# One core, latent attention with a pattern branch: two program blocks joined into one, and the first slot written in another order

## The reference

```
x = x + layernorm(attn(layernorm(x)))      # x: 1 x 1024 x 256
x = x + layernorm(ffn(layernorm(x)))
attn, main branch, 16 heads:
  q = rmsnorm(h @ q_a^T) @ q_b^T           # per head 128 "nope" + 64 rotated columns
  kv_a = h @ kv_a^T                        # 64 latent columns, 16 x 64 rotated key columns
  k_nope, v = rmsnorm(latent) @ kv_b^T     # 128 + 128 per head
  main = softmax(q k^T / sqrt(192)) v, then o_w
pattern branch, 16 heads of 16 columns:
  pattern = softmax(pq pk^T / 4) pv, then sp_o_w
out = gate0 * main + gate1 * pattern       # gates = softmax over 2
ffn: two matmuls with MXFP4-quantized weights (blocks of 32), gelu between
```

## Time and profile before

| | |
|---|---|
| median of 3 runs | 828.34 us (827.77 to 829.45) |
| the profiled execution | 828.97 us, of which span 827.1 us |
| mean granted PE clock | 0.978 of full |
| PE busy | 770.1 us (93%) |
| DVE busy | 592.9 us (72%) |
| ACT busy | 390.8 us (47%) |
| POOL busy | 437.4 us (53%) |
| DMA, all queues | 68.13 MB, mean 82 GB/s |
| POOL L968, one operation | 1280 ns |

### The profile page before, as it was taken

The page is one execution under the profiler, slowest core; times in us unless marked ns, Lnnn a source line. Parts: engine busy times, 40 slices in busy tenths (PEclk is TensorE's granted clock), DMA queues, the critical chain, the costliest instruction groups (busy, mean ns, idle before and its releaser), DMA issues. The chain is left out here.

```text
span 827.1 us, 13732 instructions
## 1 busy us (share of the span) xinstructions
PE 770.1 (93%) x5408; PEld 476.1 (58%) x5408; DVE 592.9 (72%) x673; ACT 390.8 (47%) x489; POOL 437.4 (53%) x259
## 2 busy tenths in 40 slices
PE   6869989999999999999999999999999999999984
PEld 5644555555655555565555555565655555458763
DVE  5826655757678867867785779777857699993856
ACT  4513334555555545454545455545555454540361
POOL 2334009654865485658456844784496546560233
PEclk9979999999999999999999999999999999999987
DMA  8776462015200720164025104420433303402001
GB/s 224 276 216 219 101 157 48 14 40 120 58 17 15 141 63 29 29 128 115 2 86 105 56 2 81 86 78 15 83 66 117 96 28 116 122 8 84 1 1 51
DMA packets 97796, 68.13 MB, mean 82 GB/s; under 512 B 66434, under 2 KB 76228, under 8 KB 97476
## 3 DMA queue, kind: packets, MB, share of 16 engines
q1 hardware_dynamic: 97732, 67.25, 32.0%
HBM read 41.23 MB, written 17.04 MB: 70 GB/s over the span
## 5 line engine op out<-in xcount | busy, mean ns | idle before, releaser
L1005 POOL TENSOR_TENSOR acc<-acc,em 128x1024 f32<-128x1024 f32 x96 | 239.0, 2490 | 88.6 <-ACT em L1061 88.3
L1144 DVE TENSOR_REDUCE m2p<-xb 128x2 f32<-128x1024 f32 x128 | 155.6, 1222 | 64.7 <-PE xb L1303 64.7
L1152 DVE TENSOR_REDUCE m<-xb 128x2 f32<-128x1024 f32 x128 | 155.9, 1221 | 54.8 <-PE xb L1303 54.4
L1052 ACT ACTIVATE ep<-xb 128x1024 f32<-128x1024 f32 x128 | 131.4, 1027 | 124.5 <-PE xb L1303 124.5
L1061 ACT ACTIVATE em<-xb 128x1024 f32<-128x1024 f32 x128 | 131.3, 1026 | 106.3 <-PE xb L1303 97.3
L1339 PE MATMUL pvm<-em,cpair 128*32 128x512 f32 x1024 | 136.9, 607 | 0.0
L968 POOL TENSOR_TENSOR rot<-rot,sin 128x512 f32<-128x512 f32 x32 | 41.0, 1280 | 113.3 <-DMA rot<-raw 113.3
L1303 PEld LDWEIGHTS xb<-pq,pk 49*128 49x128 f32 x256 | 23.9, 184 | 108.0 <-issue 80.0
L1005 POOL TENSOR_TENSOR acc<-em 128x1024 f32<-128x1024 f32 x16 | 41.3, 2581 | 56.0 <-PE xb L1438 50.8
L1350 PE MATMUL pvp<-ep,vp 128*32 128x512 f32 x512 | 66.7, 592 | 0.0
L1303 PE MATMUL xb<-pq,pk 49*128 49x512 f32 x256 | 64.3, 499 | 1.1 <-DVE m2p L1144 1.1
(11 more groups left out here) (272 smaller groups left out, 1278.9 us busy)
## 6 DMA issues: line engine op xcount, KB each, us to landing
rot<-raw SPq DMA_DIRECT2D x128, 64.0 KB, 2.0
pk<-spqk_d SPq DMA_DIRECT2D x48, 128.0 KB, 4.1
sums<-rec_d SPq DMA_DIRECT2D x32, 128.0 KB, 2.9
ctx_d<-ctxr SPq DMA_DIRECT2D x14, 256.0 KB, 2.1
pq<-spqk_d SPq DMA_DIRECT2D x48, 64.0 KB, 2.3
wraw<-wst_d SPq DMA_DIRECT2D x7, 384.0 KB, 5.3
em<-in_o_w SPq DMA_DIRECT2D x1, 2048.0 KB, 8.0
vp<-vp_d SPq DMA_DIRECT2D x8, 256.0 KB, 4.5
```

The costliest lines, as they stand in the source:

```text
L1005: pool.tensor_tensor(acc[:, :, :], before, em[:, j:j + 2, :], ALU.add).then_inc(added, 1)
L1052: act.activation(ep[:, j:j + 2, :], src[:, :, :], ACT.Exp, scale=PAT_SCALE).then_inc(ep_ready, 1)
L1144: dve.tensor_reduce(m2p[:, 2 * tp:2 * tp + 2, t, kt], src[:, :, :], AX, ALU.max).then_inc(x_dve, 1)
L1152: dve.tensor_reduce(m2[:, q, :, t, kt], src[:, :, :], AX, ALU.max).then_inc(x_dve, 1)
```

## The change

The streams of `prologue` and `attention` are returned as functions and run in one block, one after the other on each engine. In place of the block's end stand single waits. SBUF of the prologue is laid out in another order, so that what the stacks `pq`, `pk` overlie is free early; `xb0` now overlies the last two of the eight banks. SP's last waits of the prologue are gone, and the second `wst` store moves into `first_slot`. `FIRST` and `first_slot` have another order.

```diff
+        wqn, wall, m1, wk, w1T, xn, sp_nat, kpe_nat, wpe, qa_nat, ...   (order of allocation)
 # attention: PSUM
-        xb = [... f"xb{i}" ... for i in range(NX)]
+        xb = [... f"xb{i}" ... for i in (1, 2)]
         pvm = ...
         pvp = ...
+        xb.insert(0, ctx.enter_context(nc.psum_tensor("xb0", [P, 2, HALF], F32)))
 # SP, end of the prologue
-            sp.wait_ge(s_const, 32)
-            sp.wait_ge(sp_stored, 96)
-            sp.wait_ge(w_stored, 32)
+                elif job == ("lat1", 0):
+                    store_weights(sp, 0)
 # SP, slot 0
             def first_slot():
+                sp.wait_ge(done["sp_stored"], 96)
+                sp.wait_ge(done["pe_job"], done["index"][("pe1T", 1)] + 1)
                 load_stacks(0)
                 turn(0, ORDER[0])
                 turn(0, ORDER[1])
+                done["store_weights"](sp, 1)
+                load_minus_one(0)
+                store_pattern(0)
+                store_pattern(1)
+                sp.wait_ge(done["w_stored"], 32)
+                sp.wait_ge(done["w0_lo"], 1)
                 sp.dma_start(o_nat, ...)
                 sp.dma_start(wv, ...)
+                turn(0, ORDER[2])
                 for m in range(2):
                     sp.dma_start(spo_nat[m], ...)
-                load_minus_one(0)
                 load_weights(1)
-                store_pattern(0)
-                store_pattern(1)
-                turn(0, ORDER[2])
                 store_pattern(2)
                 turn(0, ORDER[3])
                 store_pattern(3)
...
+                main_rows(0, 0)
+                pattern_rows(0)
                 sp.wait_ge(vstored, 64)
                 load_vp(0)
                 load_minus_one(1)
 # POOL: before its memsets
+            pool.wait_ge(done["pe_job"], done["last"] + 1)
+            done["evacuated"](pool, done["last"])
+            pool.wait_ge(done["s_const"], 32)
 # ACT: before sk 0
+                        act.wait_ge(done["sp_stored"], 96)
 # DVE: before the first rc
+                    dve.wait_ge(done["s_const"], 32)
 # PE: the first three tiles n = 0, 1, 2, and the P tiles of slot 0
+                    done["evacuated"](pe, done["last"] - 6 + 2 * n)
+                            pe.wait_ge(done["w0_lo"], 1)
+                            done["evacuated"](pe, done["index"][("qm1T", i)])
+                            pe.wait_ge(done["xh_ready"], 2)
+                            pe.wait_ge(done["xl_ready"], 2)
-UNIT_FIRST = {0: 0, 2: 1, 3: 4, 1: 6}
+UNIT_FIRST = {0: 0, 2: 1, 3: 4, 1: 5}
 FIRST = [
     [("P", 0)],
-    [("P", 2)],
-    [("sk", 0), ("pm", 0), ("sv", 0)],
-    [("pm", 1), ("sk", 1), ("pm", 2)],
-    [("P", 3), ("pm", 3), ("sv", 1)],
-    [("pm", 4), ("sk", 2), ("pm", 5)],
-    [("P", 1), ("pm", 6), ("oT", 0)],
-    [("pm", 7), ("sk", 3), ("pm", 8)],
-    [("oT", 1), ("pm", 9), ("sv", 2)],
-    [("pm", 10), ("oT", 2), ("pm", 11), ("sk", 4)],
-    [("pm", 12), ("oT", 3), ("pm", 13), ("sv", 3)],
-    [("pm", 14), ("oT", 4), ("oT", 5), ("pm", 15)],
-    [("oT", 6), ("oT", 7), ("mm", 0), ("oT", 8)],
-    [("mm", 1), ("mm", 2), ("vo", 0), ("mm", 3)],
-    [("mm", 4), ("vo", 1), ("mm", 5), ("mm", 6)],
-    [("mm", 7), ("vo", 2), ("vo", 3), ("mm", 8)],
+    [("P", 2), ("sk", 0), ("pm", 0)],
+    [("sk", 1), ("pm", 1), ("sk", 2), ("pm", 2)],
+    [("sv", 0), ("pm", 3), ("pm", 4)],
+    [("P", 3), ("pm", 5), ("sk", 3)],
+    [("pm", 6), ("P", 1), ("sv", 1)],
+    [("pm", 7), ("oT", 0)],
+    [("mm", 0), ("oT", 1), ("mm", 1), ("pm", 8)],
+    [("sv", 2), ("mm", 2), ("pm", 9)],
+    [("sk", 4), ("oT", 2), ("pm", 10), ("oT", 3)],
+    [("mm", 3), ("oT", 4), ("mm", 4), ("oT", 5), ("pm", 11)],
+    [("oT", 6), ("mm", 5), ("oT", 7), ("pm", 12)],
+    [("oT", 8), ("mm", 6), ("pm", 13), ("sv", 3)],
+    [("mm", 7), ("vo", 0), ("pm", 14)],
+    [("vo", 1), ("mm", 8)],
+    [("pm", 15), ("vo", 2), ("vo", 3)],
 ]
```

More of the change, by code:

```diff
@@ L48, with prologue @@
 NW = 12
-def prologue(nc, a, d, g):
+def prologue(nc, a, d, g, sem):
     jobs = [("w1T", k) for k in range(NK)] + [("xT", k, 0) for k in range(NK)] + [("spT", 0)]
@@ L70, in sb @@
             return ctx.enter_context(nc.sbuf_tensor(name, shape, dt))
-        def sem(name):
-            return ctx.enter_context(nc.semaphore(name))
         bank = [ctx.enter_context(nc.psum_tensor(f"a_bank{i}", [P, HALF], F32)) for i in range(8)]
+        wqn = sb("wqn", [P, H, QR])
+        wall = sb("wall", [P, NP, 6, P])
+        m1 = sb("m1", [P, NT, W1])
+        wk = sb("wk", [P, H, LAT])
+        w1T = sb("w1T", [P, NK, W1])
         xn = sb("xn", [P, NT, HID])
+        sp_nat = sb("sp_nat", [P, 3, 2, HID])
+        kpe_nat = sb("kpe_nat", [P, NP, HID])
+        wpe = sb("wpe", [P, NP, 256])
         qa_nat = sb("qa_nat", [96, 2, HID])
@@ L79, in prologue @@
         gate_nat = sb("gate_nat", [2, HID])
[L80 to L87, removed]
         lnq = sb("lnq", [P, QR])
@@ L122, in prologue @@
         w0_hi = sem("w0_hi")
+        w0_lo = sem("w0_lo")
         w_stored = sem("w_stored")
@@ L144, in sp_stage, with store_weights, sync_program @@
             return hi[:, 1, half_of(h)], lo[:, 1, half_of(h)]
-        block = ctx.enter_context(nc.Block())
-        @block.sync
-        def _(sp):
+        def store_weights(sp, q):
+            n = slice(4 * q + (q == 0), 4 * q + 4)
+            evacuated(sp, index[("lat1", q)])
+            sp.dma_start(d["wst"].rearrange("n p c -> p n c")[:, n, :],
+                         wall[:, n, :, :].rearrange("p n c j -> p n (c j)")).then_inc(w_stored, 16)
+        def sync_program(sp):
             x = a["x"].rearrange("b (t p) n -> p (b t) n", p=P)
@@ L181, in _, with pool_program @@
                         sp.dma_start(d["spqk"][w, lo, 0:P, half_of(h)], t.bitcast(F32)).then_inc(sp_stored, 16)
[L182 to L187, removed]
-            sp.wait_ge(s_const, 32)
-            sp.wait_ge(sp_stored, 96)
-            sp.wait_ge(w_stored, 32)
-        @block.gpsimd
-        def _(pool):
+                elif job == ("lat1", 0):
+                    store_weights(sp, 0)
+        def pool_program(pool):
             own = [0]
@@ L221, in _, with tensor_program @@
                                    ALU.subtract).then_inc(xl_ready, 1)
-        @block.tensor
-        def _(pe):
+        def tensor_program(pe):
             def transposes(n, blocks):
@@ L315, in hi_of, with scalar_program @@
             return g[{"cT": "kyh", "qm0T": "qm0h", "qm1T": "qm1"}[job[0]]][:, half_of(job[1])]
-        @block.scalar
-        def _(act):
+        def scalar_program(act):
             for n, job in enumerate(jobs):
@@ L343, in _, with vector_program @@
                                    wall[:, 0, :, :].rearrange("p c j -> p (c j)"), ACT.Copy).then_inc(w0_hi, 1)
-        @block.vector
-        def _(dve):
+        def vector_program(dve):
             own = [0]
@@ L425, in _ @@
                     dve.wait_ge(w0_hi, 1)
-                    link(dve.tensor_tensor(wst[:, 0, 6:12, :].rearrange("p c j -> p (c j)"),
-                                           wall[:, 0, :, :].rearrange("p c j -> p (c j)"),
-                                           wst[:, 0, 0:6, :].rearrange("p c j -> p (c j)").bitcast(F32), ALU.subtract))
+                    dve.tensor_tensor(wst[:, 0, 6:12, :].rearrange("p c j -> p (c j)"),
+                                      wall[:, 0, :, :].rearrange("p c j -> p (c j)"),
+                                      wst[:, 0, 0:6, :].rearrange("p c j -> p (c j)").bitcast(F32),
+                                      ALU.subtract).then_inc(w0_lo, 1)
+        done = {"evacuated": evacuated, "index": index, "last": len(jobs) - 1, "w0_lo": w0_lo, "xh_ready": xh_ready,
+                "xl_ready": xl_ready, "w_stored": w_stored, "sp_stored": sp_stored, "s_const": s_const, "pe_job": pe_job,
+                "store_weights": store_weights}
+        return (sync_program, pool_program, tensor_program, scalar_program, vector_program), done
 def pattern_weights(g):
@@ L513, in x_steps, with attention @@
     return steps
-def attention(nc, a, d, g):
+def attention(nc, a, d, g, sem, done):
     NS = 16
@@ L530, in sb @@
             return ctx.enter_context(nc.sbuf_tensor(name, shape, dt))
-        def sem(name):
-            return ctx.enter_context(nc.semaphore(name))
         NX = 3
-        xb = [ctx.enter_context(nc.psum_tensor(f"xb{i}", [P, 2, HALF], F32)) for i in range(NX)]
+        xb = [ctx.enter_context(nc.psum_tensor(f"xb{i}", [P, 2, HALF], F32)) for i in (1, 2)]
         pvm = ctx.enter_context(nc.psum_tensor("pvm", [P, HALF], F32))
         pvp = ctx.enter_context(nc.psum_tensor("pvp", [P, HALF], F32))
+        xb.insert(0, ctx.enter_context(nc.psum_tensor("xb0", [P, 2, HALF], F32)))
         kxh, kxl, kyh, kyl = g["kxh"], g["kxl"], g["kyh"], g["kyl"]
@@ L680, in weights_at, with sync_program, load_stacks @@
             return v + 1 < NP and s == (9 if v else 13)
-        @block.sync
-        def _(sp):
-            def load_stacks(v):
```

(54 more changed lines are left out.)

## The result

The changed kernel takes 824.61 us (823.86 to 825.40, 4 runs) against 828.34 (827.77 to 829.45, 4 runs); ratio 0.9953, 95% interval 0.9933 to 0.9972. Measured again later (e11) the ratio was 0.9964 (0.9944 to 0.9983). So it is faster by 3 to 4 us; 7.3 were forecast. A kernel's time here is the median of its fast executions; one execution each of e1, of e2 and of before beside them was far slower (958 to 1230 us) and is left out. The profiled execution took 825.40 us, span 823.6 against 827.1.

The account below looks back on a forecast made before the run. PE was nearly always busy in slots 2 to 8, so only time won before slot 1 counts: `M 0` 8.3 us sooner, less 0.2 clock and 0.8 wait, gives 7.3; median 821.0, range 816.0 to 825.5.

Parts of the forecast that it names:

- Start of slot 0: At the old block boundary: `P 0` starts at 40.15, 6.5 us sooner; PE idles 0.75 us instead of 7.3, full clock.
- Stacks of pair 0: First pattern stacks in slot 0: issued at 34.7, no wait at `pm 0`; the 2.8 us wait and 1.6 of half clock go.
- PE's dense work: PE in slot 0: 51.6 us of dense work, 23.9 of it up to `oT 0`, reached at 64.1.
- SP's chain to `oT 0`: Slot 0: turns, weight store, `o_w`, queue block of 6.8, `sp_o_w`; `oT 0` at 67.0 after 2.9 us wait, `mm 0` at 68.9.
- Rival A: Queue behind `o_w` and value weights: no block, next DMA accepted at once, `T 0` 12.1 us sooner, 815.0; chance 0.12.
- `mm 0` to `T 0`: Rest of slot 0: from 68.9 to 102.4, 3.8 us of idle PE before `T 0`, `M 0` after 0.35, 8.3 sooner.
- Slot 1: After `M 0`: 0.8 us of wait at the first `pm` and 0.2 more for clock, leaving 7.3 of 8.3.
- rival B: Slot 1: pair 1's stacks come late, half clock behind; two to four us more lost, 823 to 825; chance 0.17.
- My likeliest case: The forecast as a whole: median 821.0 us; chance 0.62 for 818.5 to 823.5.
- the distance from `T 0` to the end as before within 2.5 us: Sign in the changed kernel's timeline: time from slot 1's `T 0` to the end stays within 2.5 us of before.
- Clock: Half clock behind PE's waits: 1.65 us at `oT 0`, 0.2 more in slot 1; by the skill page about 819.4.
- Rivals C and D: C (0.05): late weight store delays `o_w`, unit 3's turn and the end, slower; D (0.04): PE's start stays tied, 828.

Follow-up runs that it names:

- e11: The changed kernel measured once more, unedited; 825.93 us, ratio 0.9964.
- e1: The kernel before, two blocks and SP's program kept, with only `FIRST` and `UNIT_FIRST` of the change; 831.58 us, ratio 1.0025.
- e2: The changed kernel with `FIRST`, `UNIT_FIRST` and the place of the row transfers of before; 823.74 us, ratio 0.9926.
- e3: The changed kernel with the value weights' load moved behind the turn of unit 3, `sp_o_w` and the next weights; 824.61 us, ratio 0.9945.
- e5: e4's kernel with the first two turns of pair 1 issued ahead of the `vo` stores and the `ffn_up` load; 818.92 us, ratio 0.9884.
- e4: The changed kernel with the stacks of pair 1 loaded ahead, in slot 0, instead of in slot 1; 822.60 us, ratio 0.9912.
- e9: e6 with unit 1 one step later; SP issues pair 1's stacks, row transfers, `vp`, weights, turns, then `vo` stores and rows of -1; 810.50 us.
- e6: The changed kernel, `FIRST` reordered: load-free work ahead of `oT 0`, last maxima ahead of `vo`, row transfers to match; 820.97 us, ratio 0.991.
- e7: e6's list, with pair 1's stacks, `vp` and rows of -1 loaded ahead of the row transfers; 819.73 us, ratio 0.99.
- e8: The kernel before with only the prologue's SBUF tensors allocated in the change's order; 828.51 us, ratio 1.0.

## Why the prediction was right, and where it was not

*Start of slot 0.* Right in kind: 0.8 us of idle PE (0.75 forecast), full clock after it. It was 1.5 us later than said, 41.65 for 40.15, all of it from the prologue, which I had taken as unchanged: `P 0` waited for the same DVE copy, which itself came later. The ten profiles of joined programs start slot 0 at 40.12 to 41.76, with the median at 41.0. So some 0.7 of the 1.5 is luck of this one profile, and some 0.8 is usual: my 40.15 is their lower end.

*Stacks of pair 0.* I took no wait, with 2.4 at the other end; it was 1.2, over the 1 us that I had allowed, and the slack ahead of `oT 0` took it up. They went out at 36.10 (34.7 forecast) and PE could go on 12.4 us later, not 10.2. My worst case of 48.5 should have been 48.7 by its own rows (33.2 + 5.3 + 10.2).

*PE's dense work.* 23.9 us to `oT 0`: 41.65 + 1.2 + 23.9 is 66.7, and PE did arrive at 69.64 - 3.36 = 66.3.

*SP's chain to `oT 0`.* Right in size: wait 3.36 (2.9 forecast), at 69.64, 2.6 later than said, 1.5 of it from the start of the slot; `mm 0` at 71.52, 1.9 after `oT 0` as forecast. Its cause was half right. I laid it on the 6.8 us for which the queue took nothing. e3 took these away from the turn and won 0.7 us at `mm 0`: its DMAs land about when `o_w` does, whether they are accepted early or late. Rival A is therefore out, even where its own condition is met.

*`mm 0` to `T 0`.* 32.5 us (71.52 to 104.02) against 33.5 forecast (68.9 to 102.4); the wait was 4.12 for 3.8. `M 0` directly behind: right.

*Slot 1.* This is the term that was mis-sized: the wait for the stacks of pair 1. I wrote that SP's work at the slot's end stands "at nearly the same distance from `T 0` as before" and took 0.8 us of wait and 0.2 of clock. The distance had grown by 2.8 us: before, `vp` and the rows of -1 were out of the way before `T 0` ran; now they stand behind the row transfers, and `T 0` goes off right behind these. "10 us after `T 0` in both", which I held against rival B, was not so either: the issues ended 9.4 us after it before and 11.2 in the change. With PE some 2 us sooner at its first `pm`, as I had said, the wait was 3.71, and the half clock behind it took about 1.7 us more (4.6 us at 0.63). Together it is 5.4 in place of the 0.8 that I had for it. e5 removed that, with the wait that would have come next, and got 5.5 us back within slot 1. Rival B, at 0.17, named this mechanism and 823 to 825; that is where the time lies. My likeliest case held up to `T 0`, B from there. Luck made the miss look smaller: at U this profile is 1.95 us ahead where I had 7.3, and 1.5 us of the 3.5 come behind U, where nothing was changed. My sign "the distance from `T 0` to the end as before within 2.5 us" held (718.4 and 719.6 us) and was too wide to catch this.

*Clock.* The waits of 3.36, 4.12 and 3.71 us were each followed by about half clock (0.55, 0.57 and 0.63 in the stretches above), as were, among others, those of 2.8 and 1.97 us before and one of 2.39 us in e4 (0.70 from 124.3 to 130). But the clock stayed full behind 1.99 us in e2, at the tile where before it had fallen behind 1.97, and behind 1.22 us in the changed kernel and 1.52 and 1.43 us in e9. What the Trainium skill says of short gaps being free (TensorE: Matmul & The Clock Gate, section on HAM oscillation) thus agrees with the last four and not with 1.97, 2.8 and 2.39. The length of one wait does not settle it in these traces, and my step from a wait to a stretch of half clock rested on two rows; for the three waits that counted it came true.

*Rivals C and D* did not occur: the second weight store was issued at 50.21 and `o_w` at 56.10, 5.9 later, where 5.3 to 5.6 were forecast. SP's issues between the two follow each other without a gap, so the landing of the store alone cannot be told to have set the time of `o_w`.

What stays open: where the 1.1 us come from by which slot 3 differs between profiles; why the prologue of the joined programs ends, in the median of ten profiles, some 0.8 us later than that of before, and how much of the 0.46 us at the first matmul (below) is the joined program's own; and when a wait of about 2 us costs the clock and when not.

## What to carry to other kernels

When a barrier goes, list for the one DMA queue which transfer each engine will ask for first, and when; what was idle time behind the barrier becomes a race for places in that queue, and the loser may stand a whole slot later. Put the transfer that is asked for next ahead, however small it is, and move stores and transfers that are needed late behind it. Look at the queue and the tile list together: from the changed kernel, the queue alone won 5.7 us (e5), the list alone 3.6 (e6), the two together 14 (e9), more than joining the programs had (3 to 5). With one left as it was, the next wait took a part of what the other had won. Where PE's order is written by hand, put tiles that need none of the loads in front of the one that waits, and those that feed a small DMA several tiles ahead of the end.

## What the runs showed of the hardware that I had not expected

- Two DMAs of 8 KB (the rows of -1, each in 16 runs of 512 bytes) took from 1.17 us to 5.88 us to issue, depending on what stood before them: 3.05 behind the row transfers and `vp`, 4.6 to 5.88 behind stacks and `vp` (e7, e5, e4), 1.17 behind the `vo` stores (e9). It is not these two DMAs themselves: in e9 the weight load stood right behind `vp` and took 2.44 us, where it took 0.43 in the changed kernel.
- A small DMA accepted at once can still land late: in e3 the DMAs of a turn (64 KB each), issued by 61.8, were there at 67.4, behind 2 MB issued at 56.3 and landed at 66.1.
- The first matmul of the prologue starts at 7.50 and 7.61 us in the two kernels with the old layout, at 8.28 in the one with the new layout and two blocks, at 7.88 to 8.15 in the joined ones. One profile of each, so a hint, not a finding; at the start of slot 0 e8 is 0.24 us later than before (46.89 and 46.65), and its time is the same.
